# Four attention layers on one core: another order of all engines' steps and of the PSUM banks

## The reference

```
L0: a = softmax(x^T x);  x = (relu(gap(x) w_gap)) @ ((w_conv x) @ a) + x       # gram, mix, mid
L1: q, k, v = bn(conv1x1(x));  x = gamma * v @ softmax(q^T k)^T + x            # score, scoreT, att
L2: softmax over the 8 neighbours of relu-projections, and over channels,
    x = (1 - g) x + g * elu(h_s + h_p)                                          # near, chan, join
L3: 16 projections, 2-D Fourier transform, magnitudes summed into 90 angle bins,
    the two highest peaks choose the region that is amplified, inverse transform,
    projection back, out = x + that                                             # s1, s2, energy, pick, i1, i2, wout
```

## Time and profile before

| | us |
|---|---|
| median of three runs | 290.1 |
| profiled execution | 290.33 |
| its span, first to last instruction | 288.5 |
| TensorE busy | 272.3 (94%) |
| VectorE busy | 213.2 (74%) |
| ScalarE busy | 186.2 (65%) |
| GpSimd busy | 95.1 (33%) |

### The profile page before, as it was taken

One profiled execution on the slowest core, in us unless ns is written; L12 is line 12 of the kernel. 1 busy time (PEld: TensorE's weight loads), 2 busy tenths in 40 slices (PEclk: granted clock), 3 DMA queues, 4 the chain that ended last, 5 costly groups with the idle time before them and its releaser, 6 DMA issues.

```text
span 288.5 us, 4440 instructions
## 1 busy us (share of the span) xinstructions
PE 272.3 (94%) x1499; PEld 178.6 (62%) x1499; DVE 213.2 (74%) x325; ACT 186.2 (65%) x355; POOL 95.1 (33%) x102
## 2 busy tenths in 40 slices
PE   7999999999999899999999999799999799999994
PEld 3846555467677576747657464467867557765462
DVE  3865889789998786763489867799788775828383
ACT  0774676789997474766648776688748457674320
POOL 1045031505236878128004101354279814000000
PEclk9999999999999999999999999979999999999998
DMA  6951000000000000000000000000000000000015
GB/s 184 353 202 51 0 1 1 2 0 1 3 0 1 0 2 0 1 3 0 0 3 1 0 2 1 1 0 2 1 0 2 1 0 3 2 4 0 2 73 220
DMA packets 4520, 8.14 MB, mean 28 GB/s; under 512 B 1118, under 2 KB 2014, under 8 KB 4498
## 3 DMA queue, kind: packets, MB, share of 16 engines
q1 hardware_dynamic: 4498, 7.85, 7.8%
HBM read 5.68 MB, written 2.10 MB: 27 GB/s over the span
## 4 chain that ended last, share of the span: by engine, by line
PE 66%; DVE 10%; POOL 8%; ACT 8%; issue 3%; DMA 2%; SPq 1%; DVEq 0%; POOLq 0%; ACTq 0%
PE psum L360 64%; POOL e1h L1047 4%; ACT e L686 3%; DVE e1l L900 3%; DMA qs<-row 2%; ACT psum L677 2%; POOL ks L1040 1%; DVE nmax L884 1%; POOL qs L1037 1%; SPq L348 1%; DVE nmax L850 1%; ACT qs L669 1%; POOL regionb L1010 1%; ACT ks L670 1%; DVE x L860 1%
## 5 line engine op out<-in xcount | busy, mean ns | idle before, releaser
L1047 POOL CAST e1h<-e 128x1024 fp32r<-128x1024 f32 x32 | 42.6, 1333 | 34.7 <-ACT e L686 21.6
L900 DVE TENSOR_TENSOR e1l<-e,e1h 128x1024 fp32r<-128x1024 f32 x32 | 40.8, 1282 | 9.8 <-POOL e1h L1047 9.7
L686 ACT ACTIVATE e<-psum 128x1024 f32<-128x1024 f32 x32 | 32.8, 1025 | 20.6 <-DVE e1l L900 15.7
L850 DVE TENSOR_REDUCE nmax<-psum 128x1 f32<-128x1024 f32 x32 | 39.0, 1221 | 9.3 <-PE psum L360 8.7
L657 ACT ACTIVATE e<-psum,nmax 128x1024 f32<-128x1024 f32 x32 | 35.7, 1115 | 14.2 <-issue 9.6
L884 DVE TENSOR_REDUCE nmax<-psum 128x1 f32<-128x1024 f32 x32 | 38.0, 1217 | 3.9 <-PE psum L360 3.8
L677 ACT ACTIVATE psum<-psum,nmax 128x1024 f32<-128x1024 f32 x32 | 34.8, 1089 | 7.0 <-DVE nmax L884 6.3
L360 PE MATMUL psum<-e,v0n 128*64 128x512 f32 x128 | 31.0, 604 | 0.0
L360 PE MATMUL psum<-ks,qs 96*128 96x512 f32 (+2 forms) x96 | 30.1, 405 | 0.8 <-DVE ks L874 0.4
L360 PE MATMUL psum<-qs,ks 96*128 96x512 f32 (+2 forms) x96 | 28.9, 389 | 1.8 <-DMA qs<-row 1.3
L360 PE MATMUL psum<-xh 128*128 128x512 f32 x64 | 28.3, 442 | 0.6 <-DVE x L860 0.3
(11 more groups left out here) (175 smaller groups left out, 491.4 us busy)
## 6 DMA issues: line engine op xcount, KB each, us to landing
out<-xin SPq DMA_DIRECT2D x8, 256.0 KB, 2.1
xin<-in_x SPq DMA_DIRECT2D x3, 512.0 KB, 6.1
twist<-in_twist_in SPq DMA_DIRECT2D x1, 768.0 KB, 7.4
zz<-in_region_in SPq DMA_DIRECT2D x2, 360.0 KB, 3.5
xin<-in_x SPq DMA_DIRECT2D x2, 256.0 KB, 2.8
untwist<-in_untwist_in SPq DMA_DIRECT2D x1, 512.0 KB, 7.2
zz<-in_near_in SPq DMA_DIRECT2D x1, 288.0 KB, 4.4
rw<-in_rows_w SPq DMA_DIRECT2D x1, 256.0 KB, 2.7
```

What stands on the lines that cost most here:

```text
L686: inc(go(e1[:, E1_AT[b, i], :], t[:, :], ACT.Exp), "e1_ready", b)
L850: inc(vec.tensor_reduce(nmax0[z][:, i:i + 1], t[:, :], AX.X, ALU.max, negate=True), "nmax0_ready", b)
L900: inc(vec.tensor_tensor(e1l[:, EH_AT[b, i], :], e1[:, E1_AT[b, i], :], e1h[:, EH_AT[b, i], :].bitcast(F32), ALU.subtract), "e1l_ready", b)
L1047: done(gp.tensor_copy(e1h[:, EH_AT[b, i], :], e1[:, E1_AT[b, i], :]), "e1h_ready", b, i)
```

## The change

The four lists are replaced by four others. The same steps stand in them, with the same buffers and the same transfers. Only the fillers are fewer: warm.0.0 to warm.0.22 in place of warm.0.0 to warm.0.27. No other line is touched. A line of the diff, whose form all of it has:

```diff
-    "split.0.0 split2.0.0 split.0.1 split2.0.1 gram.0.0 pool.0.0 bn1.0.0 gram.0.1 gram.0.2 gram.0.3 norm0.0.0 "
+    "split.0.0 split2.0.0 bn1.0.0 split.0.1 split2.0.1 gram.0.0 gram.0.1 gram.0.2 norm0.0.0 gram.0.3 pool.0.0 "
```

## The result

| | before | after |
|---|---|---|
| median of the timed executions, us | 290.3 | 301.91 (300.13 to 302.04) |
| profiled execution, us | 290.33 | 300.13 |
| its span, us | 288.5 | 298.2 |

The ratio is 1.0388, 95% interval 1.0351 to 1.0425: the change makes the kernel 3.9% slower. The forecast was 289.1, with a range up to 291.2, so sign and size were both wrong. (The 290.3 is the median of four executions, one more than the 290.1 above.)

The account below looks back on a forecast made before the run. Up to 262 us TensorE's work plus its idle spots was taken to bound the kernel, then a chain of short steps. Terms summed to -0.95 from 290.33, less 0.23 to the median: 289.1 us, range 287.3 to 291.2.

Parts of the forecast that it names:

- Term 1: The start: L833, waiting for the weights ahead of the second half's split, delays xconv from 7.04 to 8.9, +1.85 us.
- rival A: At the start, the clock falls to half for 3.5 us behind the new wait, costing 1.7 us: 290.7, chance 0.25.
- Term 2: 40 to 75 us: reordered TensorE work covers idle spots such as the waits of 0.43 and 0.33, -1.5 us.
- Rival B: Term 2 is 0, the start's shift not absorbed since VectorE and ScalarE are late too: 290.6, chance 0.10.
- Term 3: 75 to 97 us: later POOL regionb and ramp gain 1.0, VectorE's lateness costs 1.1, net +0.1 us.
- Term 4: 97 to 233 us: no net change, 0 us; the two waits of 0.78 and 1.05 stay.
- Term 5: 233 to 262 us: bare wait of 0.9 for ScalarE's x2 copy, less 0.3 from nearT.3.1, +0.6 us.
- Term 6: The tail behind join.3.1: x3 steps ahead of the peak search let image 3's projection start earlier, -2.0 us.
- Rival D: The tail gives nothing, the first search starting later and its images' outputs holding VectorE: 291.1, chance 0.05.

Follow-up runs that it names:

- b_bn1_fill: The kernel before with bn1 moved ahead of the second half's split on VectorE and five fillers ahead of gram.0.0 on TensorE: 292.42 us, ratio 1.0059.
- b_bn1_ahead: The kernel before with one step moved: bn1 ahead of the second half's split on VectorE, as in the change: 296.37 us, ratio 1.0194.
- a_bn1_back: The changed kernel with one step moved: bn1 behind the second half's split on VectorE: 295.99 us, ratio 1.0175.
- a_fill: The changed kernel with five more fillers ahead of gram.0.0 in TensorE's list: ratio 1.0191.
- h_mid: The order of before, with the new order of all engines only between gram.2.0 and mid.3.1: 291.95 us, ratio 1.0036.
- h_tail_region: h_tail with POOL's regions.0.1 moved from behind e1h.0.7 to behind xkeep.0.0: 286.94 us, ratio 0.9881.
- a_bn2_early: a_bn1_back with bn2 also moved on VectorE, from behind gram.0.6 to behind gram.0.0: 292.61 us, ratio 1.0085.
- h_late: The order of before, with the new order of all engines only between mid.3.1 and join.3.1: 293.21 us, ratio 1.0099.
- h_tail: The order of before up to join.3.1, with the new order of all engines behind it: 288.48 us, ratio 0.9922.
- h_start: The new order of all engines up to gram.2.0, the order of before from there on: 301.52 us, ratio 1.0385.
- h_start_look: The same kernel as h_start, unchanged, profiled in another execution: 293.74 us, a second execution 299.98.
- a_norm_first: The changed kernel with two neighbours on VectorE exchanged, norm0.0.2 ahead of bn2: 301.93 us, ratio 1.0405.
- b_bn2_ahead: The kernel before with bn2 moved ahead of norm0.0.2, gram.0.7 and norm0.0.3 on VectorE: 295.7 us, ratio 1.0192.
- h_best: h_tail_region with POOL's xkeep.2.0 moved behind e1h.3.7 and TensorE's nearT.3.1 moved to just ahead of s2.2.0: 286.7 us, ratio 0.9865.

## Why the prediction was wrong

**Term 1 (+1.85) and rival A (290.7, chance 0.25) are the step that failed.** The wait was sized rightly: 1.8 us by b_bn1_fill against 1.85. Its parts were off both ways: xl was complete at 7.94 and not at 8.2, and the three matmuls behind it took 1.10 and not 0.7 (0.98 in before, 6.06 to 7.04), so that xconv started at 9.10 against 8.9. What comes behind it was sized at nothing. I kept the clock out of the sum because in before it fell behind one wait of 1.05 us and not behind the other of 1.01, and in the rival I took the 3.5 us of the earlier trace rows as the length. It fell for 6.83, and that cost 3.4 us at mix.0.0 by the traces and 4.0 by the timed runs (b_bn1_ahead against b_bn1_fill), twice what rival A took. The sentence of the prediction on the Trainium skill (TensorE: Matmul & The Clock Gate, "What's actually happening") pointed to the right place, and I gave it a quarter; but the clock was not late to rise, it was full from 5.00 to 8.40 and fell again. The nearest row was no bound for a wait twice as long.

**bn2 has no term.** I went through each engine's order and compared starts with wants, but took bn2 for a step of 5 us that only moves, and did not follow who stands behind it: norm0.0.2 and gram.0.7. It is worth 2.3 us of wait, and in a_bn1_back and a_fill 1.4 of clock. Its duration also was not a property of the step: 5.22 us in before, 7.32 after, 4.39 where POOL did not run its long steps beside it.

**Term 2 (-1.5) brought nothing that stayed.** TensorE is busy 34.60 of 35 us in 40 to 75, but about the same work had 34.19 in before (33 to 68 us), not the 33.12 of the earlier trace rows. Of the two waits of the earlier trace rows the 0.43 is covered and the 0.33 is 0.15. From mix.1.0 to gram.2.0 the shift went from 7.28 to 7.02 only, and h_mid shows the 0.6 gained by attH.0.1 lost again behind it. Rival B named the number, but not for its reason, engines that are late behind the start: h_mid, which is on time, loses the gain as well.

**Term 3 (+0.1)** kept within its bounds: from gram.2.0 to mid.3.1 the shift grew by 0.9. TensorE's waits there are others, and the long one of the earlier trace rows is gone. That its gain of 1.0 was real is shown by h_tail_region, that the rest of the new order more than eats it by h_mid (+1.1). That this is VectorE's lateness, as the term says, fits the waits for L676 and for the row transfer, but no run tests it alone.

**Term 4 (0) was +3.2** in the trace of the changed kernel (7.9 to 11.1), of which 1.9 are the order: so much, from scoreT.2.0 to asproj.3.0, in a_bn2_early and a_bn1_back, which have no stretch at half clock there. It was 2.2 in h_late with one stretch, and 3.3 with two in a_fill. The two waits of the earlier trace rows stayed at 0.79 and 1.05, as said. I bounded what could get worse by 1.0 and counted only POOL's sum before the last cast; the waits that are new or longer are for a bank (1.01) and for single casts on the way (1.05, 0.49).

**Term 5 (+0.6) was +0.5** from asproj.3.0 to join.3.1, and its wait, forecast at 0.9, came at 1.00.

**Term 6 (-2.0) was right**: -1.9 in the trace of the changed kernel, -2.3 in the timed runs of h_tail (ratio 0.9922, interval 0.9892 to 0.9952), and each station within 0.2 us. Rival D falls.

The sum by the traces is 4.6 (bn1) + 2.4 (bn2) + 0.9 (terms 2 and 3) + 3.2 + 0.5 - 1.9 = +9.7 us. The median is 1.8 above the profiled execution, whose mean clock of 0.977 lies among the others' 0.972 to 0.983; this remainder is open, like that of h_start.

## What to carry to other kernels

A wait that a new order puts on the busiest engine near its start is priced twice, once as a wait and once by the granted clock in the work behind it; a few fillers in its place take the second price away (292.42 against 296.37 us). When a long step moves ahead in an in-order queue, list every step that now stands behind it with its consumers: here one of them moved back ahead gained nothing (301.93 us), the long step moved further ahead, to where no long step of POOL runs beside it, gained 3.4 (292.61 against 295.99). Cut an order into stretches and time each alone: the good quarter of a bad change (here the tail) may be had without the rest.

## What the runs showed of the hardware

The granted clock at the start, by executions with bn1 ahead: behind waits of TensorE of 2.26, 2.13 and 1.98 us it was at half for 6.83 us (after, b_bn1_ahead, h_start); behind 1.56, 1.32, 0.88 and 0.57 it stayed full (h_start_look, a_norm_first, b_bn1_fill, a_fill). Later it is less regular: 2.3 us before mix.0.2 was followed by 3.41 us at half in a_bn1_back and a_fill, and by none in after, h_start and h_start_look; 3.10 us before gram.1.1 by one in a_norm_first, and 2.91 us before gram.1.0 by none in b_bn2_ahead; the 1.05 us at scoreT.2.0 by one in h_tail and by none in h_tail_region. So the length of the wait alone does not tell whether the clock falls.

What a stretch costs is not always half its length. The 6.83 us cost 3.4 at mix.0.0. The 3.41 us from 187.57 in before cost only 0.2 (h_start and h_tail_region, without it, gain 0.2 between scoreT.2.0 and asproj.3.0), those behind mix.0.2 cost 1.4, and one that came at 193.67 in b_bn1_fill 1.0 more than that of before.

Executions of one program therefore differ: those of h_start by 4.4 us in one session (297.41 to 301.84) and by 8 with h_start_look, on another chip. The 13 of the kernel before, timed beside the first, keep within 1.5; in another session one of nine took 305.64 us, at a mean granted clock of 0.85.

The weights' transfer lands at another time in each execution: ident was there at 6.1 at the earliest (h_start_look) and 7.7 at the latest (h_best) in these traces, though issued at 3.53 in every one. A wait for it moves with it.

A two-input operation of VectorE on three numbers takes 0.16 us alone, and 0.99 or 2.27 when POOL runs a step of 1.04 or 2.36 us at that time; it ends with POOL's step. It holds the other way round too: POOL's cast of 1.04 us (L1047) takes 2.00 when VectorE's two-input L900 began first and ran from 232.37 to 233.60 (second row; the first has the cast alone):

```profile
231.30 1.04 POOL L1047 CAST e1h<-e 128x1024 fp32r<-128x1024 f32 x1 [0.16 <-POOL ks L1040]
232.50 2.00 POOL L1047 CAST e1h<-e 128x1024 fp32r<-128x1024 f32 x1 [0.16 <-POOL e1h L1047]
```

The Trainium skill (SBUF — State Buffer, "SBUF: two separate sides") says that the two engines share a port pair which one instruction holds whole, and that a VectorE operation with two inputs in SBUF blocks against it, whichever starts first. By that rule, these traces agree, to 0.02 us in L772 and L774.
